# A deformable convolution's blend through PSUM, its first tile computed one stage earlier, and a straight-line sum

## The chip, the cores and the metric

The kernel runs on one core of one Trainium2 chip. The metric is the device time of one execution in microseconds (us); lower is better. The kernel before takes 6706.94 us, the median of 3 runs (6700.41 to 6711.05).

## The reference

The input is x, (2, 128, 64, 64) in fp32. It is normalised over its channels and goes through four deformable-convolution branches (7x7, 1x1, 1x1 and 3x3: 49 + 1 + 1 + 9 = 60 taps) and a pooled branch. A 1x1 convolution fuses them, and x is added. A spectral mixing layer over tokens follows, which the change doesn't touch. The part that matters, cut:

```python
def deform_conv(x, off_w, off_b, mod_w, mod_b, reg_w, k, pad):
    offset = conv2d(x, off_w, off_b, pad)
    mask = 2.0 * jax.nn.sigmoid(conv2d(x, mod_w, mod_b, pad))
    ...
    sampled = bilinear_sample(x, py, px) * mask[:, None]
    return jnp.einsum('bckhw,ock->bohw', sampled, reg_w.reshape(O, C, k * k))
# bilinear_sample: four corners, gathered at data-dependent places
    return v00 * (1 - wy) * (1 - wx) + v01 * (1 - wy) * wx + v10 * wy * (1 - wx) + v11 * wy * wx
# around it
x = x + conv_ref(ln_c(x), ...)          # ends in relu(group_norm(conv2d(cat, fuse_w)))
t = t + ffn_ref(ln_t(t), ...)           # spectral layer
```

## The kernel before, in words

The stages run one after another, with all five engines released together at the start of each.

**`stage_normalise`** takes image 0 in 8 chunks of 512 pixels. PE turns a chunk (`turn_x`), DVE measures and normalises it, PE turns it back, ACT copies it into the padded image `xnpad`. SP and ACT each issue four DMAs a chunk that write the gather table in DRAM: one row per place of a 67 x 67 grid, holding the four corner vectors of 128 fp32 each. SP also stores `xnpad` to `xn`. Ahead of that SP writes zeros to the table's border (`table<-zero`) and loads the offset weights `wom`. SP and ACT both wait for all zeros (`border_written`) before chunk 0 goes on.

**`stage_branches`** is most of the time. The work is 16 groups of 512 pixels with 60 taps each: 960 tiles, numbered n. Offsets and corner weights of a group come from a convolution of `xn`. The first group's four quarters are done alone at the start (`convolve_first(m)`, m = 0 to 3), from a window of rows reloaded from `xn` (`load_win`). Later groups are convolved between tiles. Per tile:

1. POOL issues four indirect DMAs (L477) that gather 128 table rows each into `G`, a ring of 6 buffers. It waits until the tile 6 before is blended.
2. DVE multiplies three corners by weights in PSUM (L638), and ACT multiplies the first corner in place (L512).
3. DVE adds corners 2 and 3 to corners 0 and 1 (L642, 1024 columns), then corner 1 to corner 0 (L647, 512 columns) into `acc`.
4. PE turns `acc` into `ps_t` (L759, two buffers), ACT copies it to `sT` two tiles later (L520), and PE multiplies it with the weights `R` (L771).

Every engine follows an order written out by hand. In DVE's, every 56 tiles a burst of small operations prepares the next group's offsets: `rows(m)` and `weights(m)`, four times over 8 tiles. At tap 54 `measure` (L652) takes statistics of three branches.

**`stage_sum`** is relu(fu) + x in 16 chunks, in register loops over two buffers each. `stage_fuse` ahead of it, and the token, mixture, spectral and output stages behind it, stay as they are.

Of the kernel before, what the change touches and what calls it, by code (L numbers as in the profile page):

```python
# [5 lines left out]
B, C, H, W = 2, 128, 64, 64  # L6
# [56 lines left out]
def stage_normalise(nc, x, tables, ident, eps6, xpart, xn, w_om, wom):  # L63

    ctx = ExitStack()
    with ctx:
        sb = lambda name, shape, dt=F32: ctx.enter_context(nc.sbuf_tensor(name, shape, dt))
        sem = lambda name: ctx.enter_context(nc.semaphore(name))
        BANKS = 4
        xg = [sb(f"xg{i}", [C, CH]) for i in range(GI)]  # L70
# [23 lines left out]
        wom_loaded = sem("wom_loaded")  # L94
        xn_stored = sem("xn_stored")
# [11 lines left out]
        @block.gpsimd  # L107
        def _(pool):
            pool.memset(zero[:], 0.0).then_inc(zero_set, 1)
            pool.memset(xnpad[:], 0.0).then_inc(pad_zeroed, 1)  # L110

        @block.sync
        def _(sp):
            sp.wait_ge(zero_set, 1)
            for y in (0, TS - 2):
                sp.dma_start(grid[y:y + 2, :, :].rearrange("y x s -> (y x s)").rearrange("(p n) -> p n", p=TS),
                             zero[:, :]).then_inc(border_written, 16)
            for c in (0, TS - 2):
                sp.dma_start(grid[2:TS - 2, c:c + 2, :].rearrange("y x s -> y (x s)"), zero[0:TS - 4, :])\
                    .then_inc(border_written, 16)  # L120
            sp.dma_start(wom[:], w_om).then_inc(wom_loaded, 16)
            sp.wait_ge(border_written, 64)
# [8 lines left out]
            sp.wait_ge(xn_stored, 16 * GI)  # L131
            sp.wait_ge(wom_loaded, 16)

        @block.tensor
        def _(pe):
# [11 lines left out]
            for i in range(GI):  # L147
                pe.wait_ge(xn_ready, i + 1)
                if i >= BANKS:
                    pe.wait_ge(xn_copied, i - BANKS + 1)  # L150
                for j in range(4):
                    last = nc.tensor.transpose(ps_n[i % BANKS][:, 128 * j:128 * j + 128], xt[i][:, j, :], ident[:, :])
                last.then_inc(xn_turned, 1)
                if i + BANKS < GI:
                    turn_x(i + BANKS)

# [35 lines left out]
        def _(act):  # L192
# [3 lines left out]
            act.wait_ge(border_written, 64)  # L196
# [6 lines left out]
            for i in range(GI):  # L203
                if i + 1 < GI:
# [5 lines left out]
                                     ps_n[i % BANKS][:, :].rearrange("p (y x) -> p y x", x=W), ACT.Copy)\  # L210
# [3 lines left out]
        with nc.Block() as clearing:  # L214
            @clearing.sync
            def _(sp):
                for s in x_loaded + [zero_set, border_written, pad_zeroed, x_turned, var_ready, sd_ready,
                                     dve_step, xn_ready, xn_turned, xn_copied, summed, table_written, wom_loaded, xn_stored]:
# [3 lines left out]
def stage_branches(nc, x, xn, tables, wom, base_om, bias_om, row_off, regw, ident, eps6, om_dram, y_dram, ystats, xpart):  # L222

    ctx = ExitStack()
    with ctx:
# [20 lines left out]
        R = sb("R", [C, TAPS, O])  # L246
        first_win = flat(R[:, WIN_TAP:TAPS, :])[:, 0:7 * HR * W].rearrange("c (k r x) -> c k r x", k=7, r=HR)
# [15 lines left out]
        ps_t = [ctx.enter_context(nc.psum_tensor(f"ps_t{h}", [C, CH], F32)) for h in range(2)]  # L263
        ps_w = ctx.enter_context(nc.psum_tensor("ps_w", [128, 4 * 3, HALF_TAPS], F32))
        ps_c = ctx.enter_context(nc.psum_tensor("ps_c", [128, CH], F32))
        ps_shared = ctx.enter_context(nc.psum_tensor("ps_shared", [128, CH], F32))
# [6 lines left out]
        win_loaded = pair("win_loaded")  # L273
# [51 lines left out]
        centre = 24  # L325
        conv_taps = sorted(range(49), key=lambda t: (t != centre, t))
        far = tables[1].rearrange("(y x) s -> y x s", x=TS)

        def columns(t):
            ky, kx = divmod(t, 7)  # L330
            return TAPS if 2 <= ky <= 4 and 2 <= kx <= 4 else 49
# [34 lines left out]
        def _(sp):  # L366
            for h in range(2):
                sp.sem_inc(stored[h], 16)

            def load_win(r):  # L370
                src = bass.AP(tensor=xn[0].tensor, offset=r * HP, ap=[[HP * HP, C], [1, 7], [1, W]])
                sp.dma_start(first_win[:, :, r, :], src).then_inc(win_loaded[r // 8], 16)
# [48 lines left out]
            for r in range(HR):  # L421
                load_win(r)
# [73 lines left out]
        def _(act):  # L496
# [11 lines left out]
            def corner0(n):  # L508
                g, k = divmod(n, TAPS)
                act.wait_ge(gathered[k % RING], (n // RING) * 64 + 64)  # L510
                for j in range(4):
                    last = nc.scalar.activation(G[k % RING][:, j, 0:C], G[k % RING][:, j, 0:C], ACT.Copy,  # L512
                                                scale=om[g % 2][:, j, 1, k:k + 1])
                last.then_inc(first_corner, 1)

            def copy_out(n):
# [3 lines left out]
                nc.scalar.activation(sT[n % 2][:, :], ps_t[n % 2][:, :], ACT.Copy).then_inc(copied, 1)  # L520
# [31 lines left out]
            for n in range(NT + LAG + 1):  # L552
# [7 lines left out]
                if LAG <= n < NT + LAG:  # L560
                    copy_out(n - LAG)
# [14 lines left out]
        def _(dve):  # L576
# [54 lines left out]
            def blend(n):  # L631
                g, k = divmod(n, TAPS)
                corners = lambda lo, hi: G[k % RING][:, :, lo * C:hi * C]
                three = corners(1, 4).rearrange("p j (c d) -> p j c d", c=3)
# [76 lines left out]
        def _(pe):  # L711
# [1140 lines left out]
```

## Time and profile before

| quantity | us |
|---|---|
| median of 3 runs | 6706.94 |
| profiled execution, its own time | 6683.35 |
| its span, first to last instruction | 6681.7 |
| POOL, DVE, PE busy in the span | 4168.7, 4711.9, 5252.1 |

A profile row of a group gives the source line, engine, operation, output and inputs, then the count, the busy time with the mean of one in ns, and the engine's idle time ahead of these instructions with what ended it. "issue" means that the engine waited for nothing that the profile shows. A timeline row gives the start, the duration and the instruction, and in brackets the idle time ahead of it. SPq, ACTq and POOLq are an engine's sequencer issuing a DMA.

### The profile page before, as it was taken

What the parts mean: (1) busy time and instruction counts of PE and PEld (TensorE: products, weight loads), DVE (VectorE), ACT (ScalarE), POOL (GpSimd) and SP (SyncE); (2) the same over time, 40 slices, a digit from 0 to 9 for tenths busy, and PEclk for the clock granted to TensorE, in tenths of its full rate; (3) what the DMA queues carried; (4) which work ended last, traced back from release to release, by engine and by line L of the source; (5) the groups of instructions that cost most, each with busy time, mean ns of one, the idle gap of its engine ahead of it and who ended that gap; (6) DMA issues with size and microseconds to landing.
All of it is one profiled execution on the core that took longest, in us unless ns stands there. A gap on an engine that the chain in (4) does not pass through costs nothing. (4 is left out here: it accounts for less than half of the span.)

```text
span 6681.7 us, 64757 instructions
## 1 busy us (share of the span) xinstructions
PE 5252.1 (79%) x16608; PEld 2652.2 (40%) x16608; DVE 4711.9 (71%) x5736; ACT 2586.6 (39%) x6416; POOL 4168.7 (62%) x4363
## 2 busy tenths in 40 slices
PE   4978778787887778787787878775666756999998
PEld 3433323333332333333232333322222325777777
DVE  2787877777777777777777777868776255666665
ACT  0343333333333333333333333333333542666663
POOL 1777777777777777777777777777777101222221
PEclk9999999999999989999999999998888878999999
DMA  7777777777777777777777777777776655555555
GB/s 229 209 230 212 227 218 229 219 213 209 214 211 212 214 211 215 208 207 212 215 207 215 207 224 202 218 200 217 199 210 201 230 185 197 155 146 150 149 148 181
DMA packets 593360, 1362.51 MB, mean 204 GB/s; under 512 B 108104, under 2 KB 273864, under 8 KB 591312
## 3 DMA queue, kind: packets, MB, share of 16 engines
q0 software_dynamic: 327680, 1044.66, 54.4%
q1 hardware_dynamic: 237088, 295.80, 13.9%
q10 hardware_dynamic: 28336, 19.10, 0.9%
q8 instruction: 104, 1.70, 0.1%
q14 instruction: 152, 1.25, 0.1%
HBM read 1243.49 MB, written 115.72 MB: 203 GB/s over the span
## 5 line engine op out<-in xcount | busy, mean ns | idle before, releaser
L477 POOL DMA_INDIRECT G<-table,om x3840 | 3899.1, 1015 | 1221.0 <-issue 1137.4
L512 ACT ACTIVATE G<-G,om 128x128 f32<-128x128 f32 x3840 | 1226.5, 390 | 2888.9 <-DMA G<-table,om 2888.9
L638 DVE TENSOR_TENSOR G<-G,ps_w 128x1536 f32<-128x1536 f32 x960 | 1682.0, 1752 | 928.7 <-DMA G<-table,om 912.7
L771 PE MATMUL ps_y<-sT,R 128*128 128x512 f32 x3840 | 2054.1, 663 | 48.5 <-ACT sT L520 48.3
L759 PE MATMUL ps_t<-ident,acc 128*128 128x128 f32 x3840 | 670.9, 301 | 1108.3 <-DVE acc L647 1106.8
L642 DVE TENSOR_TENSOR G<-G 128x1024 f32<-128x1024 f32 x960 | 1177.5, 1227 | 109.4 <-ACT G L512 7.2
L759 PEld LDWEIGHTS ps_t<-ident,acc 128*128 128x128 f32 x3840 | 447.7, 149 | 1855.6 <-DVE acc L647 1746.3
L771 PEld LDWEIGHTS ps_y<-sT,R 128*128 128x128 f32 x3840 | 734.0, 212 | 635.1 <-issue 559.1
L1570 DVE TENSOR_TENSOR vl<-ps_v,vh 128x512 fp32r<-128x512 f32 x1024 | 657.7, 685 | 333.6 <-ACT vh L1519 333.6
L1504 POOL DMA_DIRECT2D ut<-spec_dram x512 | 262.7, 513 | 888.6 <-PE ps_v L1585 637.0
L647 DVE TENSOR_TENSOR acc<-G 128x512 f32<-128x512 f32 x960 | 664.0, 692 | 99.2 <-DVE G L642 3.2
L741 PE MATMUL ps_shared<-xr,wom 128*52 128x512 f32 x1470 | 721.7, 611 | 0.0
L741 PE MATMUL ps_c<-xr,wom 128*128 128x512 f32 x1470 | 718.4, 609 | 0.0
L1519 ACT ACTIVATE vh<-ps_v 128x512 fp32r<-128x512 f32 x1024 | 579.6, 596 | 297.8 <-PE ps_v L1585 273.5
L520 ACT ACTIVATE sT<-ps_t 128x512 f32<-128x512 f32 x960 | 554.6, 578 | 252.8 <-PE ps_y L771 248.9
L741 PEld LDWEIGHTS ps_c<-xr,wom 128*128 128x128 f32 x1470 | 291.1, 199 | 377.1 <-issue 377.1
L1608 PE MATMUL ps_yf<-vh,mh 128*128 128x512 f32 x1024 | 413.8, 404 | 0.0
L1608 PE MATMUL ps_yf<-vh,ml 128*128 128x512 f32 x1024 | 411.5, 402 | 0.0
L1608 PE MATMUL ps_yf<-vl,mh 128*128 128x512 f32 x1024 | 409.5, 400 | 0.0
L1585 PE MATMUL ps_v<-tt,ut 96*128 96x512 f32 x1024 | 368.0, 401 | 15.1 <-DMA ut<-spec_dram 13.3
L741 PEld LDWEIGHTS ps_shared<-xr,wom 128*52 128x52 f32 x1470 | 155.6, 127 | 515.4 <-issue 515.4
L1585 PEld LDWEIGHTS ps_v<-tt,ut 96*128 96x128 f32 x1024 | 194.8, 191 | 70.8 <-DMA ut<-spec_dram 18.8
(182 smaller groups left out, 2187.8 us busy)
## 6 DMA issues: line engine op xcount, KB each, us to landing
tt<-kern_dram SPq DMA_DIRECT2D x512, 192.0 KB, 3.4
G<-table,om POOLq DMA_INDIRECT x3840, 3.7
y_dram<-yb SPq DMA_DIRECT2D x64, 512.0 KB, 4.5
yin<-y_dram SPq DMA_DIRECT2D x16, 2048.0 KB, 8.2
ut<-spec_dram POOLq DMA_DIRECT2D x256, 96.0 KB, 3.3
spec_dram<-spec_hi SPq DMA_DIRECT2D x64, 256.0 KB, 2.6
ut<-spec_dram POOLq DMA_DIRECT2D x256, 48.0 KB, 3.0
om_dram<-om_next SPq DMA_DIRECT2D x60, 150.0 KB, 3.3
```

The costliest lines, as they stand in the source:

```text
L477: pool.indirect_dma_start(G[k % RING][:, j, :], None, tables[g // GI], bass.IndirectOffsetOnAxis(ap=om[g % 2][:, j, 0, k:k + 1].bitcast(I3 ...
L512: last = nc.scalar.activation(G[k % RING][:, j, 0:C], G[k % RING][:, j, 0:C], ACT.Copy, scale=om[g % 2][:, j, 1, k:k + 1])
L638: nc.vector.tensor_tensor(three, three, ps_w[:, :, h:h + 1].to_broadcast([128, 12, C]) .rearrange("p (j c) d -> p j c d", j=4), ALU.mult). ...
L642: nc.vector.tensor_tensor(corners(0, 2), corners(2, 4), corners(0, 2), ALU.add).then_inc(added, 1)
L647: nc.vector.tensor_tensor(acc[n % 3][:, :, :], corners(1, 2), corners(0, 1), ALU.add).then_inc(blended, 1)
L741: last = nc.tensor.matmul(ps_c2 if rest else ps_c[:, :], cols[:, 128:128 + REST] if rest else cols[:, 0:128], rows, start=(tap == 0), stop ...
L759: last = nc.tensor.transpose(ps_t[n % 2][:, 128 * j:128 * j + 128], acc[n % 3][:, j, :], ident[:, :])
L771: last = nc.tensor.matmul(ps_y[:, half, :], R[:, k, 128 * half:128 * half + 128], sT[n % 2][:, :], start=(k == t0), stop=(k == ends[br] - 1))
L1519: nc.scalar.activation(vh[c][:, n, :, :], spread(ps_v[n % BANKS]), ACT.Copy).then_inc(v_high, 1)
L1570: nc.vector.tensor_tensor(vl[c][:, n, :, :], spread(ps_v[n % BANKS]), vh[c][:, n, :, :].bitcast(F32), ALU.subtract).then_inc(v_low, 1)
L1585: nc.tensor.matmul(ps_v[n % BANKS][:, :], ut[j][:, SRC[c][p], :], tt[j][:, :, :].rearrange("p r n -> p (r n)"), start=True, stop=True).the ...
L1608: last = nc.tensor.matmul(ps_y[q][:, :], m[:, c, k, :], v[c][:, :, k, :], start=(c == 0 and k == 0 and n == 0), stop=(c == 1 and k == KF - ...
```

## The change

- **Border.** The four zero writes of whole table rows become 16 writes that cover only the corner slots which `write_table` doesn't write. The zero tile shrinks, and `border_written` is waited for at the end of the stage, no longer ahead of chunk 0.
- **First tile.** POOL copies the window of the first 14 rows out of `xnpad` in SBUF (seven copies), and the convolution for m = 0 runs in `stage_normalise`, on PE behind chunk 4. The 14 loads and their waits go. `R` and `ps_shared` are allocated outside both stages, and `stage_normalise` has two `ps_n` banks in place of four.
- **Blend.** ACT writes the first corner times its weight to a PSUM tile `ps_a`, and waits until the blend before has ended, since there is one `ps_a`. DVE adds corners 1, 2 and 3 to it one at a time, 512 columns each; the last addition writes `acc`. `ps_t` has one buffer in place of two, and ACT copies it one tile later in place of two.
- **Sum.** Written out, with four buffers in place of two.

The core of the diff:

```diff
 @block.gpsimd (stage_normalise)
-  pool.memset(zero[:], 0.0)       # [TS, 2*4*C]
+  pool.memset(zero[:], 0.0)       # [TS, 2*C]
   pool.memset(xnpad[:], 0.0).then_inc(pad_zeroed, 1)
+  pool.wait_ge(pad_zeroed, 1)
+  pool.wait_ge(xn_copied, 2)
+  for kx in range(7):
+      pool.tensor_copy(first_win[:, kx, :, :], xnpad[:, 0:HR, kx:kx + W]).then_inc(first_copied, 1)
 @block.sync
-  for y in (0, TS - 2):
-      sp.dma_start(grid[y:y + 2, :, :]..., zero[:, :]).then_inc(border_written, 16)
-  for c in (0, TS - 2):
-      sp.dma_start(grid[2:TS - 2, c:c + 2, :]..., zero[0:TS - 4, :]).then_inc(border_written, 16)
+  for slot, (dy, dx) in enumerate(((0, 0), (0, 1), (1, 0), (1, 1))):
+      part = slice(slot * C, (slot + 1) * C)
+      for y0, y1 in ((0, 2 - dy), (TS - 1 - dy, TS)):
+          sp.dma_start(grid[y0:y1, :, part].rearrange("y x s -> x y s"), ...)
+      for x0, x1 in ((0, 2 - dx), (TS - 1 - dx, TS)):
+          sp.dma_start(grid[2 - dy:TS - 1 - dy, x0:x1, part], ...)
   sp.dma_start(wom[:], w_om).then_inc(wom_loaded, 16)
-  sp.wait_ge(border_written, 64)
...
+  sp.wait_ge(border_written, 256)                 # at the stage's end
 @block.tensor
+      if i == 4:
+          pe.wait_ge(first_copied, 7)
+          pe.wait_ge(wom_loaded, 16)
+          convolve_window(nc, ps_shared, first_win, wom, 0).then_inc(first_done, 1)
 @block.scalar
-  act.wait_ge(border_written, 64)
 stage_branches, @block.sync
-  for r in range(HR):
-      load_win(r)
 @block.scalar
 def corner0(n):
     act.wait_ge(gathered[k % RING], (n // RING) * 64 + 64)
+    act.wait_ge(blended, n + RING)
     for j in range(4):
-        last = nc.scalar.activation(G[k % RING][:, j, 0:C], G[k % RING][:, j, 0:C], ...)
+        last = nc.scalar.activation(ps_a[:, j, :], G[k % RING][:, j, 0:C], ...)
...
-  if LAG <= n < NT + LAG:
-      copy_out(n - LAG)
+  if 1 <= n <= NT:
+      copy_out(n - 1)
 @block.vector, blend(n)
-  nc.vector.tensor_tensor(corners(0, 2), corners(2, 4), corners(0, 2), ALU.add).then_inc(added, 1)
+  nc.vector.tensor_tensor(ps_a[:, :, :], corner(1), ps_a[:, :, :], ALU.add).then_inc(added, 1)
...
+  dve.wait_ge(added, 2 * n + 1)
+  nc.vector.tensor_tensor(ps_a[:, :, :], corner(2), ps_a[:, :, :], ALU.add).then_inc(added, 1)
   dve.wait_ge(turned, n + 1)
-  dve.wait_ge(added, n + 1)
-  nc.vector.tensor_tensor(acc[n % 3][:, :, :], corners(1, 2), corners(0, 1), ALU.add).then_inc(blended, 1)
+  dve.wait_ge(added, 2 * n + 2)
+  nc.vector.tensor_tensor(acc[n % 3][:, :, :], corner(3), ps_a[:, :, :], ALU.add).then_inc(blended, 1)
 @block.tensor
-  for m in range(AHEAD):
+  pe.sem_inc(om_done, 1)
+  for m in range(1, AHEAD):
       convolve_first(m)
 stage_sum
-  with sp.Fori(0, B) as b: ...                    # two buffers of x and of relu
+  NBUF = 4
+  for k in range(NG):
+      if k >= NBUF:
+          sp.wait_ge(t_added, k - NBUF + 1)
+      sp.dma_start(xg[k % NBUF][:, :], x[b, :, i * CH:i * CH + CH]).then_inc(x_loaded[k % NBUF], 16)
```

DVE's order at the blends of three tiles of the first group, before; G5, G0 and G1 are ring buffers, and the waits are in brackets:

```order
245 L638 TENSOR_TENSOR G5<-G5,ps_w 128x4x384 [waits weights_spread,gathered5]
246 L642 TENSOR_TENSOR G5<-G5 128x4x256 [waits weighted,first_corner]
247 L647 TENSOR_TENSOR acc2<-G5 128x512 [waits corners_added,turned]
248 L638 TENSOR_TENSOR G0<-G0,ps_w 128x4x384 [waits weights_spread,gathered0]
249 L642 TENSOR_TENSOR G0<-G0 128x4x256 [waits weighted,first_corner]
250 L647 TENSOR_TENSOR acc0<-G0 128x512 [waits corners_added,turned]
```

The same engine in the changed kernel, again in the first group:

```order
288 L663 TENSOR_TENSOR G1<-G1,ps_w 128x4x384 [waits weights_spread,gathered1]
289 L667 TENSOR_TENSOR ps_a<-G1,ps_a 128x512 [waits weighted,first_corner]
290 L671 TENSOR_TENSOR ps_a<-G1,ps_a 128x512 [waits corners_added]
291 L674 TENSOR_TENSOR acc1<-G1,ps_a 128x512 [waits corners_added,turned]
292 L663 TENSOR_TENSOR G2<-G2,ps_w 128x4x384 [waits weights_spread,gathered2]
```

Four operations stand where three stood, and each addition has one input from `G` and one from `ps_a`.

ACT in the main loop before, with the copies out of `ps_t`:

```order
123 L512 ACTIVATE G0<-G0,om0 128x128 [waits gathered0]
124 L512 ACTIVATE G0<-G0,om0 128x128 x3
125 L520 ACTIVATE sT0<-ps_t0 128x512 [waits summed,turned]
126 L512 ACTIVATE G1<-G1,om0 128x128 [waits gathered1]
127 L512 ACTIVATE G1<-G1,om0 128x128 x3
```

ACT in the changed kernel:

```order
124 L537 ACTIVATE ps_a<-G0,om0 128x128 [waits blended,gathered0]
125 L537 ACTIVATE ps_a<-G0,om0 128x128 x3
126 L545 ACTIVATE sT1<-ps_t 128x512 [waits summed,turned]
127 L537 ACTIVATE ps_a<-G1,om0 128x128 [waits blended,gathered1]
```

The first corner now also waits for `blended`, and the copy beside it is of the tile just before (sT1 beside G0).

PE at chunk 4 of the normalising stage, changed kernel (L168 turns a normalised chunk, L253 is the first convolution):

```order
25 L168 MATMUL ps_n<-ident,xt 128x128 [waits xn_copied,xn_ready]
26 L168 MATMUL ps_n<-ident,xt 128x128 x3
27 L253 MATMUL ps_shared<-wom,R 128x180 [waits wom_loaded,first_copied]
28 L253 MATMUL ps_shared<-wom,R 128x3x49 x16
...
34 L253 MATMUL ps_shared<-wom,R 128x3x49 x16
35 L168 MATMUL ps_n<-ident,xt 128x128 [waits xn_copied,xn_ready]
```

The turns of chunks 5 to 7 now stand behind 49 matmuls and their wait for `wom`.

## Rows read from the trace of the kernel before

**Rows 1.** Busy time by stage; columns PE, PEld, DVE, ACT, POOL, clock, DMA share, GB/s.

```profile
167.00:5209.00 5042.00, 3901.46 (x10780) 1621.95 (x10780) 3835.06 (x4105) 1799.04 (x5034) 3876.27 (x3817) 0.93 0.73 213
5394.00:5431.00 37.00, 0.00 (x0) 0.00 (x0) 17.55 (x16) 12.91 (x16) 0.00 (x0) 0.50 0.37 113
```

**Rows 2.** Groups of POOL's instructions from 170 to 5209.

```profile
L477 POOL DMA_INDIRECT G<-table,om x3816 | 3876.2, 1016 | 1165.5 <-issue 1131.3 <-DVE acc L647 34.2
```

**Rows 3.** The line L477: min, median and max of one gather's issue.

```profile
L477 POOL DMA_INDIRECT G<-table,om x3840: 940/946/1998, 118.9 to 5207.8; - x192
```

**Rows 4.** Timeline 1158 to 1166, POOL and DVE.

```profile
1158.79 1.23 DVE L642 TENSOR_TENSOR G<-G 128x1024 f32<-128x1024 f32 x1
1159.26 1.58 POOL L477 DMA_INDIRECT G<-table,om  x1 [0.30 <-issue]
...
1161.73 1.75 DVE L638 TENSOR_TENSOR G<-G,ps_w 128x1536 f32<-128x1536 f32 x1 [0.92 <-DMA G<-table,om]
1162.39 0.95 POOL L477 DMA_INDIRECT G<-table,om  x1 [0.30 <-issue]
1163.59 1.23 DVE L642 TENSOR_TENSOR G<-G 128x1024 f32<-128x1024 f32 x1
1163.64 1.98 POOL L477 DMA_INDIRECT G<-table,om  x1 [0.30 <-issue]
```

**Rows 5.** Groups of DVE's instructions from 170 to 5209.

```profile
L638 DVE TENSOR_TENSOR G<-G,ps_w 128x1536 f32<-128x1536 f32 x958 | 1678.5, 1752 | 921.4 <-DMA G<-table,om 905.4 <-DVE om_next L618 12.9
L642 DVE TENSOR_TENSOR G<-G 128x1024 f32<-128x1024 f32 x958 | 1175.1, 1227 | 109.2 <-ACT G L512 7.2 <-DVE G L638 3.3
L647 DVE TENSOR_TENSOR acc<-G 128x512 f32<-128x512 f32 x958 | 662.6, 692 | 99.0 <-DVE G L642 3.2
L629 DVE COPY ps_w<-omw 128x360 f32<-128x360 f32 x31 | 16.4, 528 | 0.0
```

**Rows 6.** Timeline of DVE, a burst: the multiply of three tiles.

```profile
1889.59 1.75 DVE L638 TENSOR_TENSOR G<-G,ps_w 128x1536 f32<-128x1536 f32 x1
...
1903.12 1.75 DVE L638 TENSOR_TENSOR G<-G,ps_w 128x1536 f32<-128x1536 f32 x1
```

**Rows 7.** Timeline behind the burst: two tiles in a row on DVE and PE.

```profile
1920.21 1.75 DVE L638 TENSOR_TENSOR G<-G,ps_w 128x1536 f32<-128x1536 f32 x1
1920.51 0.60 PE L759 MATMUL ps_t<-ident,acc 128*128 128x128 f32 x4
...
1924.00 1.75 DVE L638 TENSOR_TENSOR G<-G,ps_w 128x1536 f32<-128x1536 f32 x1
1924.40 0.60 PE L759 MATMUL ps_t<-ident,acc 128*128 128x128 f32 x4
```

**Rows 8.** Timeline, a steady stretch: a tile's last gather and its multiply.

```profile
2401.96 0.95 POOL L477 DMA_INDIRECT G<-table,om  x1 [0.30 <-issue]
...
2405.76 1.75 DVE L638 TENSOR_TENSOR G<-G,ps_w 128x1536 f32<-128x1536 f32 x1 [1.46 <-DMA G<-table,om]
```

**Rows 9.** Timeline of SP and ACT in the first stage.

```profile
6.34 15.36 SPq L119 DMA_DIRECT2D table<-zero  x2
36.04 1.28 ACT L200 ACT_TABLE_LOAD   x1 [36.04 <-DMA table<-zero]
80.74 0.62 SPq L129 DMA_DIRECT2D xn<-xnpad  x1
```

**Rows 10.** DMA issues from 0 to 120: KB each, us to landing.

```profile
wom<-in_w_om SPq DMA_DIRECT2D x1, 4410.0 KB, 24.7
```

**Rows 11.** Timeline 87 to 119, the second stage's start.

```profile
87.16 0.95 POOL L473 MEMSET yb<- 67x1024 f32 x1 [77.47 <-POOLq L214]
92.69 0.35 DVE L581 TENSOR_TENSOR base<-base,P 128x180 f32<-128x180 f32 x1 [16.26 <-DMA rowt<-in_row_off]
99.21 14.73 PE L723 MATMUL ps_shared<-wom,R 128*128 128x180 f32 x98 [29.38 <-DMA R<-xn]
118.85 1.15 POOL L477 DMA_INDIRECT G<-table,om  x1 [30.23 <-DVEq L621]
```

More of the change, by code:

```diff
@@ L217, in _, with columns, convolve_window, stage_branches @@
                 for s in x_loaded + [zero_set, border_written, pad_zeroed, x_turned, var_ready, sd_ready,
-                                     dve_step, xn_ready, xn_turned, xn_copied, summed, table_written, wom_loaded, xn_stored]:
+                                     dve_step, xn_ready, xn_turned, xn_copied, summed, table_written, wom_loaded, first_copied, first_done, xn_stored]:
                     sp.sem_clear(s)
-def stage_branches(nc, x, xn, tables, wom, base_om, bias_om, row_off, regw, ident, eps6, om_dram, y_dram, ystats, xpart):
+def columns(tap):
+    ky, kx = divmod(tap, 7)
+    return TAPS if 2 <= ky <= 4 and 2 <= kx <= 4 else 49
+def convolve_window(nc, ps_shared, first_win, wom, m):
+    centre = 24
+    taps = sorted(range(49), key=lambda t: (t != centre, t))
+    out = ps_shared[:, 0:3 * TAPS].rearrange("p (a t) -> p a t", a=3)
+    for tap in taps:
+        ky, kx = divmod(tap, 7)
+        last = nc.tensor.matmul(out[:, :, 0:columns(tap)],
+                                first_win[:, kx, 2 * m + ky:2 * m + ky + 2, :].rearrange("c y x -> c (y x)"),
+                                wom[:, tap, :, 0:columns(tap)], start=(tap == centre),
+                                stop=(tap == taps[-1]), skip_group_check=True)
+    return last
+def stage_branches(nc, x, xn, tables, wom, R, ps_shared, base_om, bias_om, row_off, regw, ident, eps6, om_dram, y_dram, ystats, xpart):
     ctx = ExitStack()
@@ L262, in stage_branches @@
         ps_y = ctx.enter_context(nc.psum_tensor("ps_y", [128, 2, CH], F32))
-        ps_t = [ctx.enter_context(nc.psum_tensor(f"ps_t{h}", [C, CH], F32)) for h in range(2)]
+        ps_t = ctx.enter_context(nc.psum_tensor("ps_t", [C, CH], F32))
+        ps_a = ctx.enter_context(nc.psum_tensor("ps_a", [128, 4, C], F32))
         ps_w = ctx.enter_context(nc.psum_tensor("ps_w", [128, 4 * 3, HALF_TAPS], F32))
         ps_c = ctx.enter_context(nc.psum_tensor("ps_c", [128, CH], F32))
-        ps_shared = ctx.enter_context(nc.psum_tensor("ps_shared", [128, CH], F32))
         ps_c2 = ps_shared[0:REST, :]
@@ L519, in copy_out @@
                     act.wait_ge(summed, n - 1)
[L520 removed]
+                nc.scalar.activation(sT[n % 2][:, :], ps_t[:, :], ACT.Copy).then_inc(copied, 1)
             def evacuate(g, br):
@@ L755, in turn @@
                 pe.wait_ge(blended, n + 1 + RING)
-                if n >= 2:
-                    pe.wait_ge(copied, n - 1)
+                if n >= 1:
+                    pe.wait_ge(copied, n)
                 for j in range(4):
-                    last = nc.tensor.transpose(ps_t[n % 2][:, 128 * j:128 * j + 128], acc[n % 3][:, j, :], ident[:, :])
+                    last = nc.tensor.transpose(ps_t[:, 128 * j:128 * j + 128], acc[n % 3][:, j, :], ident[:, :])
                 last.then_inc(turned, 1)
@@ L1021, in stage_sum @@
         sem = lambda name: ctx.enter_context(nc.semaphore(name))
-        xg = [sb(f"t_xg{h}", [C, CH]) for h in range(2)]
-        rb = [sb(f"t_rb{h}", [C, CH]) for h in range(2)]
-        pair = lambda name: [sem(f"{name}{h}") for h in range(2)]
-        x_loaded = pair("tx_loaded")
-        relu_ready = pair("relu_ready")
-        t_added = pair("t_added")
+        NBUF = 4
+        xg = [sb(f"t_xg{h}", [C, CH]) for h in range(NBUF)]
+        rb = [sb(f"t_rb{h}", [C, CH]) for h in range(NBUF)]
+        x_loaded = [sem(f"tx_loaded{h}") for h in range(NBUF)]
+        relu_ready = sem("relu_ready")
+        t_added = sem("t_added")
         block = ctx.enter_context(nc.Block())
-        NH = GI // 2
         NC = CH // (2 * S)
@@ L1068, in stage_tokens @@
+            for k in range(NG):
+                b, i = divmod(k, GI)
+                dve.wait_ge(x_loaded[k % NBUF], 16 * (k // NBUF) + 16)
+                dve.wait_ge(relu_ready, k + 1)
+                nc.vector.tensor_tensor(accum[:, 2 * b:2 * b + 2, :, i * NC:i * NC + NC], by_block(rb[k % NBUF]),
+                                        by_block(xg[k % NBUF]), ALU.add).then_inc(t_added, 1)
+            dve.wait_ge(t_added, NG)
 def stage_tokens(nc, ident, eps5, accum, uT, dft, dft_edge, spec_dram):
```

104 lines of the change are left out of this document (39 added, 65 removed).

## The prediction, made before the changed kernel was run

> **What bounds the kernel now.** I read the busy time by stage first. The main loop, 167 to 5209 us, is 5042 of 6682 us; in it POOL, DVE and PE are all about 77% busy, so the shares don't name the bound [rows 1]. The groups of POOL do: 3816 gathers take 3876.2 us, 1016 ns each, with 1165.5 us idle ahead of them. Of that, 1131.3 us are "issue" and only 34.2 us are put down to DVE's blends [rows 2]. POOL issues one gather behind the other, every 1.32 us, 5.28 us a tile, and waits for nobody. DVE waits 905 us for the gathered data [rows 5]. So the loop lasts as long as POOL takes to issue, and faster blending alone would give nothing.
>
> The mean of 1016 ns hides two kinds of gather. The median is 946 ns and the maximum 1998 [rows 3]. The timeline says which are long. At 1159.26 a gather starts while L642 runs (1158.79 to 1160.02) and ends at 1160.84; at 1163.64 another starts 0.05 us into L642, which ends at 1164.82, and ends at 1165.62. Both end 0.8 us behind L642's end, wherever they began. A gather that starts during L638 takes its plain 0.95 us [rows 4]. Both operations write `G`; they differ in their inputs: L642 reads two from SBUF, L638 one from SBUF and one from PSUM. I read it so: soon after its start a gather needs something in SBUF (the row numbers in `om`) that it can't get while DVE reads two SBUF inputs.
>
> **The main loop.** The change takes away L642 and L647 and puts in three additions with one SBUF input each. If the reading holds, the average gather falls from 1016 to 946 ns: 3816 x 0.070 = 267 us. The 0.305 us between gathers (1165.5 / 3816) stays, so a tile becomes 4 x 1.251 = 5.00 us.
>
> The Trainium skill (SBUF — State Buffer, "Who interferes with whom") says that a VectorE instruction with two SBUF inputs contends with a GpSimd instruction that reads SBUF, not with one that only writes. By that the stall goes with this change. The same list reports that `tensor_tensor` was seen not to stall a DMA, and infers that writing descriptors needs only the write port. By that half the loop would gain nothing. The two gathers of 1.58 and 1.98 us beside L642 speak against the second half here.
>
> What is late next? DVE. Its blend was 1.75 + 1.23 + 0.69 us and two gaps of 0.1: 3.88. An addition of 512 columns took 692 ns (L647). The trace has no addition that reads and writes PSUM. From below it is 692 ns. From above I take L642's 1227 ns, twice the columns. Near it stand L638, whose PSUM input shows nothing beyond 152 ns over its 1536 columns at 0.96 per ns (L642 and L647: 160), and L629, a copy into PSUM with 153 ns over its 360 columns [rows 5]. I take 0.69: the new blend is 1.75 + 3 x 0.69 + 3 x 0.1 = 4.13 us, 0.25 more. Back to back, before did a tile in 3.79 us (1920.21 to 1924.00) [rows 7]; now 4.05.
>
> That is hidden as long as POOL doesn't run into the ring of 6. In a steady stretch a tile's multiply starts 2.85 us behind its last gather [rows 8]. So the buffer is free 2.85 + 4.13 us behind it, and POOL wants it 5 x 5.00 + 0.3 us behind it: 18.3 us to spare (20.0 before). A burst of offset work uses it up: two tiles took 13.53 us (1889.59 to 1903.12) [rows 6]; with 0.5 more they fall 4.0 us behind POOL's 10.0, and four such pairs cost 16. About 2 us stay. Behind the burst DVE regains 5.00 - 4.05 = 0.95 us a tile, so it is level again after 17 of the 56 tiles. PE follows: its turns stand 3.89 us apart there [rows 7], and it is busy 3901 / 960 = 4.06 us a tile on average, under 5.0. Where a burst meets the branch statistics or image 1's normalising, POOL will wait a little. I charge 5 us in all (bounds 0 and 40, the latter if each of 14 bursts costs 3).
>
> The other new waits. The first corner waits for the blend before. In a steady stretch DVE is idle then, and in a backlog ACT's four operations, 1.3 us, lie beside L638's 1.75. Behind that wait on ACT stands the copy out of `ps_t`, for which PE's next turn waits; it comes at 1.3 + 0.6 us into the tile, and the turn is due at 4.1. One `ps_t` costs nothing by that; in stretches at PE's lower clock level (the mean granted clock is 0.93 [rows 1]) PE is late and the cover shrinks, which is part of the 40. The loop gives 267 - 5 = 262 us.
>
> **The first tile.** The second stage starts at 87.16, has its base table at 93.0 and its first convolution at 99.21 to 113.9; the first gather is issued at 118.85 [rows 11]. With the convolution done, gathers start 4.8 us behind the base table: 10.7 us into the stage, not 31.7. The later quarters follow at their old distance, less about 1 us if the first of them now meets PE's lower clock. That is 20 us (bounds 15 and 21).
>
> **The first stage.** Before, nothing goes past chunk 0 until the zeros are written at 36.04, and the last store is issued at 80.74 [rows 9]; the next stage starts 6.4 us behind it. Now chunks start at about 10 us. But PE stops at chunk 4 for `wom`, which landed 24.7 us behind its issue at 21.7, at 46.4 [rows 10], then convolves for 14.7 us, and chunks 5 to 7 can't be turned before; two chunks' writes (some 5 us each) and 6.4 us of landing follow. With `wom` where it was: 46.4 + 14.7 + 10 + 6.4 = 77.5, a gain of 10. But the zeros are now 16 writes in pieces of 512 bytes ahead of `wom` on SP's queue, and already before the second pair held SP for 15.36 us [rows 9]. I let `wom` land 8 us later, about a quarter more of the zeros' 30 us: 86, a gain of 1 (bounds -9 and 10).
>
> The Trainium skill (DMA: Bandwidth & Descriptors, "Why a DMA increments its semaphore by 16 and not by 1") gives the reason that zeros are slow: a DMA is cut over as many engines, up to 16, as divide its outermost dimensions, and 67 has no such divisor, so it goes through one engine. By that the eight writes of 67 places stay on one engine, with more pieces; no row here shows an engine by itself.
>
> **The sum.** 37 us, of which DVE is busy 17.55 [rows 1]: each pair waits for a load that could not be issued earlier. With four buffers DVE goes through 16 additions of 1.10 us behind a first landing of 3.5: 21 to 23 us. Gain 14 (bounds 8 and 16).
>
> **The sum of all.** 262 + 20 + 1 + 14 = 297. The profiled execution, 6683.35 us, would be 6386; the median of the runs lies 23.6 above that execution, and I carry this over: 6706.94 - 297 = 6410.
>
> **The rivals.**
> 1. *The stall is not the second SBUF input* but any addition on `G`, or a lock of another kind. For it: no row shows a gather starting within L647, which has two SBUF inputs too. Against it: rows 4. The loop gains nothing, the edges still 35 minus a few: about 6675. Chance 0.09.
> 2. *The handover between ACT and DVE becomes the bound.* With one `ps_a`, the first corner queues on ACT behind a copy that waits for PE, and PE's lower clock makes the copy late. A tile of 5.15 us in place of 5.00: 960 x 0.15 = 144 given back, 6554. For it: two more waits in the ring. Against it: the slack above. Chance 0.07.
> 3. *Slower than before: additions in PSUM cost far more.* The place is DVE's two in-place additions (and the third's input). DVE's other work in the loop is 3835 / 960 - 3.67 = 0.32 us a tile, so with gaps it has 4.45 of 5.00 us. From +0.55 us a tile DVE is the bound; from 5.33 us a tile (5.28 and the 35 us of the edges back) the kernel is slower, that is from three additions of 0.98 us each. At the upper bound of 1.227 a tile is 6.06 us and the time 6707 + 960 x 0.78 - 35 = 7421. L638 and L629 speak against it. Chance 0.03.
> 4. *The edges lose*: `wom` comes so late that the first stage ends at 110 us or more. It takes 25 from the gain, no more; it is inside the range.
>
> **How the numbers follow.** The forecast has 0.81. Its own range is 6372 to 6470: the loop 262 less 35 or plus 5, the edges 35 less 20 or plus 12, and 20 either way for the step between profile and median, not all at once. Rivals 1 to 3 lie outside, 0.19 together, and the range stays there. A change of 0.2%, 13 us, is about what a measurement of this kernel can tell from no change. Forecast and rivals 1 and 2 are all faster by more: 0.96. Within 0.2% 0.01, slower 0.03.
>
> **What would show it.** Right: gathers of mean 946 to 955 ns, 5.0 us a tile, additions of about 0.69 us with a PSUM input, DVE's wait for data down from 905 us to some 500; first gather at about 97 us; the sum in 22. Wrong: gathers still at 1016 ns (rival 1), POOL idle over 0.3 us with releaser `acc` all over the loop (rival 2 or 3, and the additions' mean tells which), or a first stage well past 90 us.

## The result, and the profile after

The changed kernel takes 6400.92 us (median of 4 runs, 6397.70 to 6402.89), the kernel before 6707.06 beside it (6700.41 to 6711.05). The ratio is 0.9545, 95% interval 0.953 to 0.956. Forecast were 6410 and 6372 to 6470. The profiled execution of the changed kernel took 6402.89, its span 6401.2. Beside the experiments below, one execution of the kernel before took 11934.98 us at a mean granted clock of 0.48; it is left out of every ratio and counts only in the median of 6703.89.

Busy time by stage, changed kernel; the first two rows answer to [rows 1], the last two are the token and mixture stages, which the change doesn't touch:

```profile
160.00:4937.00 4777.00, 3860.25 (x10772) 1596.07 (x10772) 3972.51 (x5062) 1849.87 (x5027) 3610.34 (x3816) 0.93 0.76 225
5121.00:5142.00 21.00, 0.00 (x0) 0.00 (x0) 16.80 (x16) 12.70 (x16) 0.00 (x0) 0.50 0.63 200
5142.00:5228.00 86.00, 55.56 (x200) 30.86 (x200) 62.75 (x239) 29.53 (x69) 0.10 (x1) 0.83 0.74 273
5228.00:5342.00 114.00, 72.77 (x400) 59.48 (x400) 52.47 (x90) 15.35 (x31) 0.00 (x0) 0.79 0.53 205
```

The loop got 264 us shorter, though DVE is busy for 137 us more in it: POOL's 3816 gathers take 266 us less, and DVE's wait for their data (L663, L638 before) falls from 905 to 446 us. Groups from 163 to 4937 us, against [rows 2, 5], and the whole line of the gather, against [rows 3]:

```profile
L501 POOL DMA_INDIRECT G<-table,om x3816 | 3610.5, 946 | 1167.2 <-issue 1147.9 <-DVE acc L674 19.4
...
L663 DVE TENSOR_TENSOR G<-G,ps_w 128x1536 f32<-128x1536 f32 x958 | 1677.9, 1751 | 462.0 <-DMA G<-table,om 446.2 <-DVE om_next L643 13.3
L667 DVE TENSOR_TENSOR ps_a<-G,ps_a 128x512 f32<-128x512 f32 x957 | 666.4, 696 | 129.7 <-ACT ps_a L537 30.7 <-DVE G L663 3.7
L671 DVE TENSOR_TENSOR ps_a<-G,ps_a 128x512 f32<-128x512 f32 x957 | 665.0, 695 | 31.7
L674 DVE TENSOR_TENSOR acc<-G,ps_a 128x512 f32<-128x512 f32 x957 | 657.6, 687 | 102.7 <-DVE ps_a L671 4.1
...
L537 ACT ACTIVATE ps_a<-G,om 128x128 f32<-128x128 f32 x3828 | 1188.9, 357 | 1802.0 <-DMA G<-table,om 1120.0 <-DVE acc L674 681.5
```

```profile
L501 POOL DMA_INDIRECT G<-table,om x3840: 942/946/1158, 108.4 to 4936.2; - x192
```

The mean gather now is the median gather, 946 ns; the maximum fell from 1998 to 1158. The gap ahead of one is still 0.306 us (1167.2 / 3816). An addition with one input in PSUM takes 687 to 696 ns. The timeline shows a gather that starts in the middle of an addition (2403.83, inside L671) and stays plain, against [rows 4]:

```profile
2402.58 0.94 POOL L501 DMA_INDIRECT G<-table,om  x1 [0.30 <-issue]
2402.76 0.70 DVE L667 TENSOR_TENSOR ps_a<-G,ps_a 128x512 f32<-128x512 f32 x1
2403.49 0.69 DVE L671 TENSOR_TENSOR ps_a<-G,ps_a 128x512 f32<-128x512 f32 x1
2403.83 0.95 POOL L501 DMA_INDIRECT G<-table,om  x1 [0.31 <-issue]
2404.29 0.69 DVE L674 TENSOR_TENSOR acc<-G,ps_a 128x512 f32<-128x512 f32 x1
```

From the 25th on, 1674 gathers of this trace start inside one of the three additions; the longest of them takes 974 ns.

The first stage, SP and PE, against [rows 9, 10]:

```profile
4.59 2.68 SPq L131 DMA_DIRECT2D table<-zero  x2
7.32 5.57 SPq L134 DMA_DIRECT2D table<-zero  x2
...
33.95 5.12 SPq L134 DMA_DIRECT2D table<-zero  x2
39.11 0.60 SPq L137 DMA_DIRECT2D wom<-in_w_om  x1
...
53.09 15.83 PE L253 MATMUL ps_shared<-wom,R 128*128 128x180 f32 x98 [25.80 <-DMA wom<-in_w_om]
...
80.82 0.61 SPq L144 DMA_DIRECT2D xn<-xnpad  x1
```

Issuing the 16 zero writes holds SP for 34.5 us; `wom` leaves 17 us later than before and lands 13.8 us after that. PE waits 25.8 us for it and still finishes in time: POOL's first instruction of the next stage starts at 87.08, as before (87.16). Its start, against [rows 11], and the DMAs that it issues first:

```profile
87.22 0.33 SPq L447 DMA_DIRECT2D R<-in_regw  x1
...
87.46 0.45 ACTq L522 DMA_DIRECT2D P<-in_bias_om  x1
87.94 0.45 ACTq L524 DMA_DIRECT2D rowt<-in_row_off  x1
...
103.23 0.35 DVE L606 TENSOR_TENSOR base<-base,P 128x180 f32<-128x180 f32 x1 [24.36 <-DMA rowt<-in_row_off]
104.07 15.95 PE L253 MATMUL ps_shared<-wom,R 128*128 128x180 f32 x98 [31.57 <-DVEq L616]
108.43 1.16 POOL L501 DMA_INDIRECT G<-table,om  x1 [19.90 <-DVEq L646]
```

```profile
R<-in_regw SPq DMA_DIRECT2D x1, 4480.0 KB, 14.5
P<-in_bias_om ACTq DMA_DIRECT2D x1, 90.0 KB, 14.5
rowt<-in_row_off ACTq DMA_DIRECT2D x1, 32.0 KB, 15.3
```

The first gather comes 10.4 us earlier than before (108.43 against 118.85), not 21: two small tables, `P` and `rowt`, land with the 4480 KB of `R` (the third, `base`, takes 2.6 us).

### The profile page after: what moved, and what is told of

Same layout as the page of the kernel before. It is cut to its first block and busy times, and to the rows that moved or that the text cites. A ratio compares the mean times of both kernels' runs of the same rounds, so it can differ in the third digit from the quotient of the medians.

```text
span 6401.2 us, 66500 instructions
## 1 busy us (share of the span) xinstructions
PE 5219.2 (82%) x16608; PEld 2633.4 (41%) x16608; DVE 4849.9 (76%) x6696; ACT 2640.8 (41%) x6416; POOL 3908.6 (61%) x4370
## 5 line engine op out<-in xcount | busy, mean ns | idle before, releaser
L501 POOL DMA_INDIRECT G<-table,om x3840 | 3633.4, 946 | 1215.2 <-issue 1154.0
L788 PE MATMUL ps_y<-sT,R 128*128 128x512 f32 x3840 | 2028.1, 656 | 24.0 <-ACT yb L553 23.8
L663 DVE TENSOR_TENSOR G<-G,ps_w 128x1536 f32<-128x1536 f32 x960 | 1681.4, 1751 | 468.2 <-DMA G<-table,om 452.4
L537 ACT ACTIVATE ps_a<-G,om 128x128 f32<-128x128 f32 x3840 | 1192.6, 357 | 1812.8 <-DMA G<-table,om 1130.6
L776 PEld LDWEIGHTS ps_t<-ident,acc 128*128 128x128 f32 x3840 | 433.6, 147 | 1665.9 <-DVE acc L674 1554.6
L545 ACT ACTIVATE sT<-ps_t 128x512 f32<-128x512 f32 x960 | 572.2, 596 | 1109.0 <-PE ps_y L788 1106.7
L1580 DVE TENSOR_TENSOR vl<-ps_v,vh 128x512 fp32r<-128x512 f32 x1024 | 656.9, 686 | 335.0 <-ACT vh L1529 335.0
L667 DVE TENSOR_TENSOR ps_a<-G,ps_a 128x512 f32<-128x512 f32 x960 | 668.5, 696 | 131.0 <-ACT ps_a L537 31.8
L674 DVE TENSOR_TENSOR acc<-G,ps_a 128x512 f32<-128x512 f32 x960 | 659.7, 687 | 103.0 <-DVE ps_a L671 4.1
L671 DVE TENSOR_TENSOR ps_a<-G,ps_a 128x512 f32<-128x512 f32 x960 | 667.1, 695 | 31.8
```

Of the source, the lines that this page charges most:

```text
L501: pool.indirect_dma_start(G[k % RING][:, j, :], None, tables[g // GI], bass.IndirectOffsetOnAxis(ap=om[g % 2][:, j, 0, k:k + 1].bitcast(I3 ...
L537: last = nc.scalar.activation(ps_a[:, j, :], G[k % RING][:, j, 0:C], ACT.Copy, scale=om[g % 2][:, j, 1, k:k + 1])
L663: nc.vector.tensor_tensor(three, three, ps_w[:, :, h:h + 1].to_broadcast([128, 12, C]) .rearrange("p (j c) d -> p j c d", j=4), ALU.mult). ...
L667: nc.vector.tensor_tensor(ps_a[:, :, :], corner(1), ps_a[:, :, :], ALU.add).then_inc(added, 1)
L671: nc.vector.tensor_tensor(ps_a[:, :, :], corner(2), ps_a[:, :, :], ALU.add).then_inc(added, 1)
L674: nc.vector.tensor_tensor(acc[n % 3][:, :, :], corner(3), ps_a[:, :, :], ALU.add).then_inc(blended, 1)
```

## The experiments

All times are medians beside the kernel before on the same chip. There were three sets, each on a chip of its own. The kernel before took 6702.80 beside the blend alone, the sum in SBUF, one addition of three and the tables ahead of `R`; 6703.89 beside the fourth addition, the split border with its control, and both; 6697.64 beside the last control pair and the plain DMAs.

**The blend alone.** The kernel before with the new blend and its copy of `ps_t`, and with the old border, first tile and sum.

```diff
 kernel before
-  ... corners(0, 2) += corners(2, 4); acc = corners(1, 2) + corners(0, 1)
+  ... ps_a += corner(1); ps_a += corner(2); acc = corner(3) + ps_a
```

> The kernel before with the new blend alone (first corner in PSUM, three additions, one ps_t); border, first tile and sum as before. If the gathers' stall beside L642 is what the blend takes away, the main loop gives 264 us and the edges (7 us of the opening and 16 of the sum in the changed kernel's trace) are missing: 6424 us, 6415 to 6435, gathers of mean 946 ns. Rival: the edges hide more than their traces show, or the blend needs them (less DMA or SP work beside it): then above 6440.

Measured: 6433.16 (6430.06 to 6434.02), ratio 0.9589 [0.9573, 0.9605]. This is inside the range, near its upper end. The loop takes 4782.6 us from gather 25 to the last, before 5037.3. By the medians the blend is 270 of the 306 us. The changed kernel's trace is 31 us shorter than this one: 7 at gather 25, 10 in the loop, where a plain gather took 948 ns in this execution (below), and 14 behind it, 16 in the sum less 2 in the rest.

**The same additions with the sum in SBUF.** This keeps the changed kernel's order, its lengths and its waits, and gives each addition its second SBUF input back. The first corner and the running sum are also written to SBUF; only for the last addition, L674, is the place of one input all that differs.

```diff
-  nc.vector.tensor_tensor(ps_a[:, :, :], corner(1), ps_a[:, :, :], ALU.add)
+  nc.vector.tensor_tensor(corner(0), corner(1), corner(0), ALU.add)
   ... likewise corner 2, and corner 3 into acc; ACT multiplies corner 0 in place
```

> The changed kernel with the same three additions of 512 columns in the same order and with the same waits, but the first corner and the running sum stay in G, so that each addition reads two inputs from SBUF. Only the place of one input differs. If two SBUF inputs hold a gather back, the long gathers come back, ended 0.8 us behind an addition: mean of 1000 ns or more, 6600 to 6720 us. Rival (it was the length of L642, 1024 columns, or the order): gathers stay at 946 ns and the time at 6401, within 10.

Measured: 6696.50 (6690.20 to 6710.69), ratio 0.9992 [0.998, 1.0003]. The whole gain of the blend is gone.

```profile
L501 POOL DMA_INDIRECT G<-table,om x3840 | 3929.1, 1023 | 1214.1 <-issue 1162.0
...
L667 DVE TENSOR_TENSOR G<-G 128x512 f32<-128x512 f32 x960 | 666.0, 694 | 115.2 <-ACT G L537 14.0
L674 DVE TENSOR_TENSOR acc<-G 128x512 f32<-128x512 f32 x960 | 664.6, 692 | 102.9 <-DVE G L671 4.1
```

DVE's additions are as long as in PSUM (692 and 694 ns), and the gathers rise to 1023 ns. The timeline shows two, each held until 0.82 us behind the addition in which it starts:

```profile
2400.70 0.69 DVE L674 TENSOR_TENSOR acc<-G 128x512 f32<-128x512 f32 x1
2401.11 1.10 POOL L501 DMA_INDIRECT G<-table,om  x1 [0.30 <-issue]
...
2404.86 0.69 DVE L671 TENSOR_TENSOR G<-G 128x512 f32<-128x512 f32 x1
2405.02 1.36 POOL L501 DMA_INDIRECT G<-table,om  x1 [0.31 <-issue]
```

The cleanest pair is L674: it writes `acc` in SBUF in both kernels, and only here holds a gather. 2401.11 + 1.10 is 0.82 behind 2401.39, and 2405.02 + 1.36 is 0.83 behind 2405.55. In this trace 392 gathers that start inside L674 take over 985 ns; in the changed kernel 679 start inside it, and none does. It isn't the length of an operation, nor `G` as its output: L663 writes `G` for 1.75 us, and of the changed kernel's 1438 gathers that start inside it none takes over 958 ns.

**One addition of three in SBUF.** Corner 2 is added to corner 3 in `G`, and `acc` takes corner 3.

```diff
-  nc.vector.tensor_tensor(ps_a[:, :, :], corner(2), ps_a[:, :, :], ALU.add)
+  nc.vector.tensor_tensor(corner(3), corner(2), corner(3), ALU.add)
```

> The changed kernel with one of its three additions reading two SBUF inputs: corner 3 takes corner 2 in SBUF, then the last addition takes corner 3 and ps_a. If such an addition holds gathers back for as long as it runs, one of 0.69 us meets the start of a gather in at most 0.69 / 1.25 = 55% of the tiles and costs 0.35 us on average: 0.19 us a tile, 180 us, so 6580; since gathers and blends keep step, anything from 6410 to 6650, with every long gather ended 0.8 us behind that one addition. Rival (length): 6401.

Measured: 6551.89 (6549.02 to 6564.47), ratio 0.9772 [0.9753, 0.9791].

```profile
L501 POOL DMA_INDIRECT G<-table,om x3840 | 3787.1, 986 | 1214.0 <-issue 1152.3
...
L671 DVE TENSOR_TENSOR G<-G 128x512 f32<-128x512 f32 x960 | 667.8, 696 | 31.8
```

None, one and three such additions a tile give gathers of 946, 986 and 1023 ns and loops of 4773, 4926 and 5068 us. The first costs more than a third. Gathers that start inside such an addition, with at least 0.13 us of it left, are 551 with one a tile and 1118 with three: the number that is hit doesn't grow in proportion. That this is so because a gather's start depends on when the last one was let go is argued, not shown. In both traces each of them, but for the few that start in the addition's first 0.045 us, ends 0.81 to 0.84 us behind the addition.

**A fourth addition in PSUM.** Corner 2 is added twice, which makes DVE's tile 0.72 us longer and leaves the gathers alone. It puts rival 3's condition, a longer tile on DVE, to the test. Rival 2, a late handover between ACT and DVE, had no run of its own. The output holds corner 2 twice.

```diff
+  nc.vector.tensor_tensor(ps_a[:, :, :], corner(2), ps_a[:, :, :], ALU.add).then_inc(added, 1)
```

> The changed kernel with corner 2 added twice, to measure DVE's margin; the output holds it twice. One addition and its wait cost 0.8 us a tile. DVE was at 4.13 us of blend and 0.32 of other work a tile beside POOL's 5.00, so it becomes the bound at 5.2 to 5.25: 190 to 240 us slower, 6590 to 6640 us, with POOL idle behind acc. Rival: waits on ACT and PE already fill the gap, then over 6700; or the additions overlap more than their gaps tell, then below 6500.

Measured: 6573.94 (6572.31 to 6578.24), ratio 0.9811 [0.9792, 0.9831], 5.18 us a tile. The line of its gather, engine idle ahead of it by releaser:

```profile
L501 POOL DMA_INDIRECT G<-table,om x3840: 940/946/1157, 109.3 to 5106.6; - x192
...
  issue: 1127.6, 3701
  DVE acc L676: 217.0, 135
```

And DVE's multiply in the whole trace, in the changed kernel idle for 468.2 us, of which 452.4 for the gathers' data:

```profile
L663 DVE TENSOR_TENSOR G<-G,ps_w 128x1536 f32<-128x1536 f32 x960 | 1677.6, 1748 | 27.3 <-DVE om_next L643 12.6
```

This is what a bound by DVE looks like: gathers stay at 946 ns, POOL waits 217 us for the blend (19.4 in the changed kernel), nearly all of it in the tiles behind a burst, and DVE hardly waits for data. It cost 175 us beside the changed kernel on the same chip (6399.02), less than the 190 to 240 expected, since the addition costs 0.72 us and not 0.8. The prediction had DVE at 4.45 us a tile; with 0.72 more that is 5.17, where 5.18 were measured. So its margin of 0.55 us a tile stands.

**The tables ahead of `R`.** SP waits for `base`, `P` and `rowt` before it issues `R`.

```diff
+  sp.wait_ge(params, 48)
   sp.dma_start(R[...], regw[...])
```

> The changed kernel with one wait more: SP loads R in the second stage only when the three small tables of ACT's queue have landed. In the changed kernel they landed 14.5 and 15.3 us behind their issue, behind R's 4480 KB, where before they took 4.0 and 4.6. If R's load is the cause, DVE's base table is ready some 10 us sooner and everything behind it too: first gather at about 98 us and 6391 us (6387 to 6394). Rival: they wait for something else at the stage's start, or the convolution of the next tile takes the gain back at PE's lower clock: 6398 to 6401.

Measured: 6401.74 (6400.82 to 6404.42), ratio 0.9545 [0.9529, 0.9561].

```profile
90.60 0.35 DVE L607 TENSOR_TENSOR base<-base,P 128x180 f32<-128x180 f32 x1 [10.76 <-DMA rowt<-in_row_off]
91.44 6.79 PE L253 MATMUL ps_shared<-wom,R 128*128 128x180 f32 x32 [18.75 <-DVEq L617]
95.79 1.16 POOL L502 DMA_INDIRECT G<-table,om  x1 [7.25 <-DVEq L647]
```

The cause was right: `base` comes 12.6 us earlier, and so does the first gather. But the time, expected at 6391, didn't fall, and the trace's loop was 9 us longer. The plain gather took 948.0 ns in this execution and 945.7 in the changed kernel's; over 3816 that is 9 us. So both kernels ran again, unchanged, on one chip.

> The changed kernel again, as the control of the next one on the same chip: 6400 us, within 6.

> The kernel with R's load held until P, the row table and the column table have landed, now beside a control on the same chip. Its first gather starts 12.6 us earlier than the changed kernel's, and gather 25 by 10.2. If the opening's gain is kept by the loop, this runs 8 to 12 us under the control. Rival: the gain is eaten, because a loop that starts earlier meets the same later limit (PE's or the ring's catching up behind the bursts, not POOL's issuing): then it runs 0 to 3 us under. The mean of the plain gathers (945 to 948 ns from one execution to another, 2.5 ns being 10 us) says how far one profile can be trusted for this.

Measured: control 6408.92 (6402.57 to 6411.68), tables first 6400.82 (6396.79 to 6402.71). In both sets the tables' median is within 1 us of 6401, and the changed kernel's was 6400.92, 6399.02 and 6408.92 on three chips. Beside its control the edit is worth 8.1 us, though the two ranges just touch. The two profiled executions are level (6402.57 and 6402.16): the plain gather again took 948.2 ns with the edit and 945.3 without. That the edit itself makes it longer isn't ruled out by this pair; other kernels without the edit read 948 too (the blend alone, the sum in SBUF), and with both edits, below, it was 946.5.

**The border in 64 and 3 places.** The zero writes of 67 places are split; the bytes and the places written stay.

```diff
-  sp.dma_start(grid[y0:y1, :, part]..., zero[:, ...])
+  for xa, xb in ((0, 64), (64, TS)):
+      sp.dma_start(grid[y0:y1, xa:xb, part]..., zero[0:xb - xa, ...])
```

> The changed kernel with each of the eight zero writes over 67 places cut into one over 64 places and one over 3. In the changed kernel's trace SP issues zeros from 4.6 to 39.1 us, and only then wom and its table writes. If writes over 67 places go through one DMA engine (67 has no divisor up to 16, 64 has 16), the zeros are issued by about 20 us, wom lands by 40, and the second stage starts at 72 to 79 us, not 87: 8 to 13 us under the changed kernel on this chip. Rival: the number of 512-byte pieces is what holds SP, or the table writes fill the DMA engines anyway: start at 84 or later, 0 to 3 us.

> The changed kernel itself, beside the next three on one chip. In the run with the tables first, a gather's plain duration read 948 to 949 ns in place of 946, which over 3840 gathers is as much as the 10 us that its opening gained; if that is the chip and not the edit, this kernel reads 946 to 949 here too and 6398 to 6412 us, and the others are to be held against it.

Measured: 6382.65 (6381.09 to 6384.60), control 6399.02 (6396.61 to 6408.66): 16.4 us, more than the 8 to 13 expected. SP's queue:

```profile
4.49 2.30 SPq L132 DMA_DIRECT2D table<-zero  x4
6.83 1.25 SPq L136 DMA_DIRECT2D table<-zero  x2
...
19.09 0.82 SPq L139 DMA_DIRECT2D wom<-in_w_om  x1
...
67.27 0.72 SPq L146 DMA_DIRECT2D xn<-xnpad  x1
```

24 writes leave in 14.5 us, where 16 took 34.5. L134's writes, of 64 places each, are the same in both kernels; a pair of them held SP for 3.3 to 6.5 us and now for 1.1 to 1.4. So SP isn't slow at its own issue; it stands behind what is queued ahead. `wom` is issued 20 us earlier, and the next stage starts 13.5 us earlier (at 73.6). The other 3 us are within what the stages behind the sum vary by from trace to trace (below). The Trainium skill (DMA: Bandwidth & Descriptors, "Why a DMA increments its semaphore by 16 and not by 1") has it that an outer dimension is cut over as many engines, up to 16, as divide it; 67 has no such divisor, 64 has. The trace agrees. These are the packets, MB and share of the 16 engines' time of SP's queue, q1, from 23.5 to 30 us in the changed kernel and from 9 to 17 us here:

```profile
q1 hardware_dynamic: 142, 0.07, 3.6%
q1 hardware_dynamic: 1307, 0.56, 25.2%
```

3.6% of 16 engines is 0.6 of one engine, and no two of the 142 packets overlap in time; 25.2% is four.

**Both.** Tables first and the split border.

> The border split as in e5_border_split, and R loaded behind the three small tables as in e4_tables_first. The two act in different stages, so they should add: 10 us (8 to 12) under e5_border_split, about 20 under the changed kernel on this chip, some 6380 us. Rival: PE's lower clock or the ring takes the tables' 10 us back: level with e5_border_split.

Measured: 6378.68 (6372.71 to 6380.29), ratio 0.9515 [0.9495, 0.9534]. It is the fastest version, 20.3 us under its control. The tables give 4.0 here, where 8 to 12 were expected. The first gather does come 12.9 us earlier than with the split border alone (82.2 against 95.1), the 25th 8.8, and the loop takes 5.4 us more. So 8.1 and 4.0 are what two pairs say of this edit, and where the rest of its 12.6 us goes stays open.

**Plain DMAs beside an operation with two SBUF inputs.** Far behind the loop POOL issues 512 direct DMAs beside DVE's L1580, which has one input in PSUM. Here both are in SBUF (the low halves of `v` become zero).

```diff
-  nc.vector.tensor_tensor(vl[c][...], spread(ps_v[n % BANKS]), vh[c][...].bitcast(F32), ALU.subtract)
+  nc.vector.tensor_tensor(vl[c][...], vh[c][...].bitcast(F32), vh[c][...].bitcast(F32), ALU.subtract)
```

> The changed kernel with one edit far behind the loop: DVE's subtraction in the spectral stage (L1580, 512 columns, in flight while POOL issues that stage's 512 plain, direct DMAs ut<-spec_dram at L1514) takes both of its inputs from SBUF in place of one from PSUM; its output no longer is the reference's. Nothing before that stage changes. Theory (what a two-input operation holds back is the gather's own reading of its row numbers from SBUF, which a plain DMA has not): L1514 keeps its mean of 513 ns, also where it starts inside L1580, and the time stays within 5 us. Rival (the operation holds back any DMA that POOL issues, since its descriptors must be written): an L1514 that starts inside L1580 ends behind it, so some of the 512 get up to 0.5 us longer, the maximum passes 1.0 us and the group's busy time of 262.6 us grows by 20 to 130 us.

Measured: 6405.60 (one run; the changed kernel's control on this chip 6408.92). The two lines:

```profile
L1514 POOL DMA_DIRECT2D ut<-spec_dram x512: 514/514/558, 5348.6 to 6304.3; - x171
```

```profile
L1580 DVE TENSOR_TENSOR vl<-vh 128x512 fp32r<-128x512 f32 x1024 | 659.7, 688 | 332.2 <-ACT vh L1529 332.1
```

Of the 512, 347 start inside L1580; their mean is 514 ns and their maximum 531, and the other 165 have the same mean. Nothing is held. In the changed kernel, with one input in PSUM, 339 start inside it, with a mean of 513 and a maximum of 528. So what is held in a gather is something that it has beyond a plain DMA. The row numbers that it reads from SBUF are such a thing, and this is the reading on which the prediction rested; that it is these and no other part of a gather's issue is argued, not shown.

## Why the prediction was right, point by point

- **The stall and its cause: right.** The loop fell by 264.2 us between the two traces, 262 were forecast. In the trace before, 705 gathers passed 985 ns, by 265 us over the median of 946 in all; 699 of them start inside L642. After, 21 do, by 1.8 us. The two gathers of [rows 4] stand for all: 984 start inside L642. Of these 28 start in its first 0.045 us and are plain, 800 end 0.81 to 0.84 us behind its end, and 156 start so near its end that they are no longer for it. Where L642 begins within 0.3 us behind a gather's start (368 times), the gather is plain too, 958 ns at most. So what counts is whether the operation is running when the gather starts, a little less than the prediction's "soon after its start". The runs with none, one and three additions with two SBUF inputs turn the stall on and off by the place of the sum alone, which rules out rival 1's "any addition on `G`". For that rival the prediction said that no row shows a gather starting within L647: seven do, all in its last 0.03 us, where nothing could be seen. On plain DMAs the Trainium skill's observation that `tensor_tensor` doesn't stall a DMA (SBUF — State Buffer, "Who interferes with whom") agrees with the 514 ns; on indirect ones it doesn't hold, as the 800 show.
- **The additions' price: right.** Forecast 0.69 us, measured 687 to 696 ns. Two tiles back to back start 3.98 us apart (4.05 forecast):

```profile
1920.99 1.74 DVE L663 TENSOR_TENSOR G<-G,ps_w 128x1536 f32<-128x1536 f32 x1
1924.97 1.75 DVE L663 TENSOR_TENSOR G<-G,ps_w 128x1536 f32<-128x1536 f32 x1
```

- **The ring: right.** POOL waits for the blend 48 times, 19.4 us, of which 48 x 0.305 is the usual gap: 5 us, as forecast. All the idle time ahead of the gathers grew by less, from 1165.5 to 1167.2 us. ACT waits 681.5 us for `ps_a`, and DVE waits 30.7 us for ACT. Rival 3's condition wasn't met; the fourth addition shows what it would have been. Against rival 2 stand the 30.7 us and the tile of 5.00 us.
- **The first tile: the mis-sized term.** Forecast 20, measured 10.4 at the first gather and 7.3 at the 25th. The step that failed is the one that took the base table at its old distance from the stage's start. It was 5.5 us, and it became 16.1, because taking the 14 window loads off SP's queue also took away what had held `R` back. Holding `R` behind the tables brought 12.6 of them back. Another 3 us (1 forecast) went at the next quarter's convolution: 15.95 us at a granted clock of 0.81, against 12.98 us at 1.00 before.
- **The first stage: right, close to luck.** Forecast 1, measured 0.1. `wom` was issued 17 us later and landed 11 sooner after its issue, so at 52.9, where 54.4 was forecast; the two shifts happened to leave it near, and the convolution took 15.8 us for 14.7. Rival 4's end at 110 us didn't come.
- **The sum: right.** From the first load to the last addition 20.5 us (forecast 21 to 23), 36.6 before: 16 against 14.
- **Left out: the stages behind the sum.** There the kernels are the same, and the changed one takes 1258.8 us to its end, the one before 1250.5. Some 6 us of the loss are in the token and mixture stages, where the granted clock is lower than before in the same work, by the same view:

```profile
5431.00:5514.00 83.00, 52.56 (x200) 29.36 (x200) 62.51 (x239) 29.34 (x69) 0.11 (x1) 0.88 0.76 278
5514.00:5625.00 111.00, 70.49 (x400) 57.85 (x400) 52.44 (x90) 15.40 (x31) 0.00 (x0) 0.82 0.56 214
```

In the rows of after it is 0.83 and 0.79. The other traces help a little: the same stages take 1257.2 us with the new blend and the old sum, 1252.8 to 1257.3 with the other edits, and 1258.8, 1261.4 and 1260.4 in three executions of the changed kernel. So it isn't the shorter sum alone, and one trace of the kernel before can't say how much of the 8 us is the change. What sets it is open.

**The sum of all: right, partly by two errors that offset each other, which is luck.** By the traces the gain is 264.2 in the loop, 7.3 at the 25th gather (the first stage's 0.1 is in it), 1.3 between loop and sum, 16.1 in the sum, less 8.3 behind it: 280.6, and the spans differ by 280.5; 297 were forecast, 17 too much. By the medians it is 306, 26 more. That is the step from profile to median: I carried 23.6 us over to the changed kernel, whose profiled execution lies 2 us above its median. The runs of the kernel before spread over 6682.6 to 6718.2 in the three sets, those of the changed one over 6396.6 to 6411.7. It fits that the length of a stall depends on how two engines' rhythms happen to meet, and that without it the executions are more alike; the kernel with the sum in SBUF spreads over 20 us again. That is argued, not shown.

Two slips in the working of the prediction change nothing: the old blend adds up to 3.87 us, not 3.88, and the tile from which the kernel is slower to 5.32 us, not 5.33.

## What to carry to other kernels

Split a mean into its kinds before pricing it: a median of 946 beside a mean of 1016 and a maximum of 1998 ns was the whole case, and the timeline beside the long ones pointed to the cause. On a path where POOL issues indirect DMAs without a pause, give DVE at most one SBUF input per operation, even at the price of more and longer work on DVE, as long as it stays under POOL's rhythm. And when loads are removed from a queue, ask what they had held back: here it was a large one, with which two small ones then landed that everybody waited for.

## What was unexpected of the hardware

- ACT's multiply of 128 columns takes 357 ns into PSUM; in SBUF, in the kernel before, 387 to 390.
- Zeros of 33 to 67 KB a write, 0.8 MB in all, held SP's queue for 34.5 us and with it a load of 4.4 MB that lands in 13.8. The shape of the write decided it, not its bytes.
- A gather's plain issue takes 945.3 to 948.2 ns from one execution to another, even for the same kernel (945.3, 945.7 and 946.6 in three executions of the changed one). It stays within 0.6 ns all through an execution, and at 3816 in a row it moves the time by up to 11 us. What sets it is open.
